# Patch tokens, two attentions and two mixtures of experts on one core: the turn to the second mixture laid out anew, LayerNorm factors in three parts, weight loads on another queue

## The reference, cut to what matters

```python
def reference(x, ...):                      # x: 128 images of 64 x 1000
    h = gelu(unfold(x, patch=(64, 25), stride=(64, 12)) @ tok_w + tok_b)   # 82 tokens of 64
    h = h + relu_attention(layernorm(h))    # causal, relu(q k^T) / row count
    h = h + moe6(layernorm(h))              # router MLP, top 2 of 6, three-layer experts
    h = h + rope_attention(layernorm(h))    # causal softmax, rotary part
    h = h + moe8(layernorm(h))              # top 2 of 8, out = tokens + sum of c_e * expert_e
    return h

def layernorm(x, eps=1e-5):
    return (x - mean(x)) / sqrt(var(x) + eps)

def moe8(tokens):
    rw, re = top_k(softmax(tokens @ router_w.T), 2)
    rw = rw / rw.sum(-1)
    return tokens + sum(combine[:, e] * (gelu(tokens @ w1[e] + b1[e]) @ w2[e] + b2[e]) for e in range(8))
```

## Time and profile before

| | us |
|---|---|
| median of 3 runs | 668.27 (664.47 to 670.48) |
| profiled execution | 667.97, its span 666.2 |
| TensorE busy | 591.1 (89% of the span) |
| VectorE busy | 505.0 (76%) |
| ScalarE busy | 297.6 (45%) |
| GpSimd busy | 148.0 (22%) |
| mean granted TensorE clock | 0.959 of full |

### The profile page before, as it was taken

How to read it: one execution, slowest core, us unless ns; L and a number is a source line. 1 busy time by engine, 2 the same in 40 slices (tenths; PEclk the granted TensorE clock), 3 DMA queues, 4 the chain that set the end, 5 groups by cost and what they waited for, 6 DMA issues and landing times.

```text
span 666.2 us, 17580 instructions
## 1 busy us (share of the span) xinstructions
PE 591.1 (89%) x6943; PEld 369.3 (55%) x6943; DVE 505.0 (76%) x1493; ACT 297.6 (45%) x716; POOL 148.0 (22%) x151
## 2 busy tenths in 40 slices
PE   1899999899998799999988889999967879999883
PEld 1885655468887344445443358777764444444441
DVE  3657779848785769888787548878887888988863
ACT  0010010023334466776775648887852434545441
POOL 1000000853655103221011041531421122121000
PEclk9999999999989799999998999999975899999997
DMA  9999883000000000000000000000000000000001
GB/s 296 411 384 331 292 292 132 2 1 1 2 1 2 1 1 1 3 1 1 2 1 1 1 2 1 1 2 2 1 1 1 7 16 22 22 22 21 20 22 25
DMA packets 28898, 39.19 MB, mean 59 GB/s; under 512 B 19985, under 2 KB 20369, under 8 KB 28817
## 3 DMA queue, kind: packets, MB, share of 16 engines
q1 hardware_dynamic: 19232, 35.46, 15.0%
q10 hardware_dynamic: 9584, 2.61, 2.0%
HBM read 35.37 MB, written 2.69 MB: 57 GB/s over the span
## 4 chain that ended last, share of the span: by engine, by line
PE 55%; DVE 24%; issue 7%; ACTq 6%; ACT 5%; DMA 2%; SPq 0%; DVEq 0%
PE bank L1522 8%; PE bank L403 7%; ACTq L1192 6%; DVE m_hm L1783 4%; PE bank L1560 4%; PE bank L1042 2%; PE bank L1558 2%; PE bank L1583 2%; PE bank L992 2%; PE bank L1006 2%; PE bank L1543 2%; PE bank L785 2%; PE bank L771 2%; DVE cols L446 2%; PE bank L1532 2%
## 5 line engine op out<-in xcount | busy, mean ns | idle before, releaser
L558 POOL TENSOR_TENSOR centred<-h,mean 82x512 f32<-82x512 f32 x64 | 72.8, 1137 | 447.3 <-DVE rstd L541 236.9
L1403 ACT ACTIVATE m_h<-bank,m_b 128x656 f32<-128x656 f32 x112 | 90.5, 808 | 115.6 <-PE bank L1522 115.4
L403 PE MATMUL bank<-cols,tok_weight 64*64 64x328 f32 (+1 forms) x1800 | 114.8, 410 | 20.2 <-DVE cols L447 18.3
L1783 DVE TENSOR_TENSOR m_hm<-bank,m_h 128x656 f32<-128x656 f32 x112 | 93.7, 836 | 34.3 <-PE bank L1532 33.0
L403 PEld LDWEIGHTS bank<-cols,tok_weight 64*64 64x64 f32 x1800 | 75.4, 135 | 55.1 <-issue 17.5
L1522 PE MATMUL bank<-m_xt,m_w 64*64 64x328 f32 x896 | 92.5, 485 | 5.9 <-ACT m_h L1403 5.0
L446 DVE COPY cols<-image 128x1992 f32<-128x1992 f32 x32 | 62.0, 1945 | 16.9 <-DMA image<-in_x_dram 14.8
L1558 PE MATMUL bank<-m_hm,m_wo 64*64 64x328 f32 x512 | 49.3, 455 | 2.7 <-DVE m_osb L1790 2.3
L1522 PEld LDWEIGHTS bank<-m_xt,m_w 64*64 64x64 f32 x896 | 24.8, 137 | 45.8 <-issue 23.2
L952 ACT ACTIVATE sa_prob<-sa_masked,sa_low 82x82 f32<-82x82 f32 x128 | 44.6, 350 | 11.3 <-DVE sa_low L1094 11.2
L381 ACT ACTIVATE tok_fm<-bank,tok_bias 128x328 f32<-128x328 f32 x16 | 7.6, 532 | 88.9 <-PE bank L403 63.1
(11 more groups left out here) (170 smaller groups left out, 1026.0 us busy)
## 6 DMA issues: line engine op xcount, KB each, us to landing
image<-in_x_dram SPq DMA_DIRECT2D x32, 1000.0 KB, 11.1
out_dram<-m_fin SPq DMA_DIRECT2D x16, 164.0 KB
tok_weight<-in_L_tok_weight_dram ACTq DMA_DIRECT2D x2, 400.0 KB, 8.1
m_w<-in_L_ffn_w_dram ACTq DMA_DIRECT2D x2, 128.0 KB
m_sel_raw<-c_sel_dram ACTq DMA_DIRECT2D x1, 256.0 KB
m_w<-in_L_ffn_expert_w_dram ACTq DMA_DIRECT2D x2, 96.0 KB
m_wo<-in_L_ffn_expert_w_dram ACTq DMA_DIRECT2D x4, 48.0 KB
m_sel_raw<-c_sel_dram ACTq DMA_DIRECT2D x1, 192.0 KB
```

The costliest lines, as they stand in the source:

```text
L403: return pe.matmul(sum_bank[u % 2][s][t * D:(t + 1) * D, L * j0:L * j1], weight[s * R:(s + 1) * R, c, :], cols[u % 2][s * R:(s + 1) * R, c ...
L558: pool.tensor_tensor(self.centred[:], slots(self.h, g), mean.broadcast_to([L, G, D]), ALU.subtract).then_inc(self.shifted, 1)
L1403: act.activation(h1[n % RING][:], h1_bank, ACT.Gelu if last else ACT.Relu, bias=W.b1[:, k:k + 1]).then_inc(h1_ready, 1)
L1783: dve.tensor_tensor(hm[k][:], cb_bank, src[n % RING][:], ALU.mult).then_inc(hm_ready, 1)
```

## The change

Nothing that is computed changes but the Newton steps' form. In words:

1. **Loads**: both mixtures' weight DMAs (54) go from ScalarE's queue to SyncE's, behind all image loads. `prepare` of both goes to VectorE's unit 7, ahead of `store(6)`.
2. **LayerNorm**: `scale` in three parts (groups 0 to 7, 8 to 11, 12 to 15), 14 instructions each, one third-order step and one Newton step, some without a wait. Every group counts by itself. In R and S the parts are spread over more groups; M does parts 1 and 2 of its own and 0 and 1 of S's; N does parts 1 and 2 of its own.
3. **Boundary S to N**: N's early turns go to banks 0, 2, 3, 2, 0 and wait for S's last `copy_qk`; the queues are interleaved anew; `copy_p` of the last group goes to ScalarE; S's last three groups' statistics go into N.
4. **Routing in N**: another `ROUTE`, and a `FIRST_ROUTE` for group 0.

```diff
@@ build
-            norm.append(LayerNorm(..., norm[-1] if i else None))
+            norm.append(LayerNorm(..., norm[-1] if i else None, (NG // 2, 3 * NG // 4, NG)))
@@ scalar queue
                 for f in range(3):
                     go(n, 1)
                     go(s, 2)
+                go(n, 1)
                 go(s)
                 go(n)
@@ tensor queue
                 go(s, 2 * (NG - 3) + 1)
                 go(n, 1)
                 go(s, 2)
+                for _ in range(2):
+                    go(n, 1)
+                    go(s, 1)
                 go(n, 1)
-                go(s, 1)
-                go(n, 1)
-                go(s, 1)
+                go(s, 2)
                 go(n, 1)
                 go(s, 1)
                 go(n, 1)
@@ vector queue
                 go(s, 2 * (NG - 2) + 1)
                 go(n, 1)
+                go(s, 3)
+                go(n, 1)
                 go(s, 1)
-                go(n, 1)
-                go(s, 2)
                 go(n, 1)
@@ stage_patches
         in_groups(step)
+        for W in moe:
+            W.load(sp)
...
-            for W in LOAD_IN.get(u, ()):
-                (*attn, *moe)[W].load(act)
+            if u == 0:
+                for W in attn:
+                    W.load(act)
...
+            if u == NU - 1:
+                for W in moe:
+                    W.prepare(dve)
             if u >= 1:
                 store(u - 1)
...
-            if u in PREPARE_IN:
-                moe[PREPARE_IN.index(u)].prepare(dve)
-            if u in (4, 5):
+            if u in SCALE_IN:           # (5, 6)
                 go(scale, 3)
+        go(following.scale(dve, 1))
@@ LayerNorm.scale(self, dve, part)
+        dve.wait_ge(self.counted, end)
         if self.previous is not None:
-            dve.wait_ge(self.previous.normed, NG if half else NG // 2)
+            dve.wait_ge(self.previous.normed, end)
+        self.mark(q = stats2 + EPS * D + stats5)
         self.link(d = even - odd)
+        yield
+        self.mark(mean = -0.5 * d + even)
         self.link(var = d * n * n / D / D * d)
         self.link(var = q / D + var)
         yield
         (two bit instructions on d)
+        yield
+        self.link(q = d * d); self.link(q = q * var)
+        yield
+        self.link(q = (q - 10/3) * q); self.link(d = (q + 5) * d)
+        yield
+        self.link(q = d * d); self.link(q = q * -0.5 * 0.375**3 * var); rstd = (q + 1.5 * 0.375) * d
@@ stage_relu_attention (vector); the rope attention has 1 <= g <= 6 in place of 2 <= g <= 7
-            if 1 <= g <= 3:
-                go(scale_mine, 2)
-            if 9 <= g <= 10:
-                go(scale_next, 3)
+            if 2 <= g <= 7:
+                go(scale_mine, 1)
+            if 9 <= g <= 11:
+                go(scale_next, 2)
@@ stage_rope_attention
+        copy_p(NG - 1)                                  # scalar, last
-                pe.wait_ge(S.behind.x_ready, g + 5 - NG)
+                pe.wait_ge(S.behind.x_ready, 1)
             if g == NG - 2:
+                yield
                 score(NG - 1)                           # tensor
         turn_p(NG - 1)
+        yield
         mix(NG - 1)
             if g == NG - 1:
                 copy_p(NG - 2)                          # vector
+                yield
-            if exists(g - 2):
+            if 2 <= g < NG - 2:
                 statistics(g - 2)
-        copy_p(NG - 1)
-        statistics(NG - 2)
@@ stage_moe
     if last:
-        ROUTE = {(0, 0): (1, 2), (0, 1): (3,), (0, 2): (4,), (1, 0): (5, 6), (1, 1): (7,), (1, 3): (0,)}
+        ROUTE = {(0, 0): (1,), (0, 1): (2,), (0, 3): (3, 4), (1, 0): (5,), (1, 1): (6, 7), (1, 3): (0,)}
+        FIRST_ROUTE = {(0, 0): (0,), (0, 1): (1, 2), (0, 3): (3, 4)}
+        SCALE_MINE, SCALE_NEXT = ({(0, 2): 2, (1, 2): 2, (2, 2): 2}, {(3, 2): 2, (4, 3): 2, (5, 2): 2}), ()
+        COUNT = {(0, 3): NG - 2, (2, 3): NG - 1}
     else:
+        SCALE_MINE = {(g, k): 1 for g in (1, 2) for k in range(NP)}, {(g, k): 1 for g in (4, 5) for k in range(NP)}
+        SCALE_NEXT = {(g, k): 1 for g in (10, 11, 12) for k in (0, 1)}, {(g, k): 1 for g in (NG - 2, NG - 1) for k in range(NP)}
+        COUNT = {(0, LAST): NG - 1}
...
-        return back if last and f <= FRONT else front
+        return psum[:, (0, 2, 3, 2, 0)[f], :] if last and f <= FRONT else front
...
-                pe.wait_ge(before.scaled, NG - 4 + f)
-                wait(pe, x_ready, f)
+                if f in (0, FRONT):
+                    pe.wait_ge(before.scaled, NG if f else NG - 4)
+                elif f < 3:
+                    pe.wait_ge(before.qk_ready, NG)
+                else:
+                    pe.wait_ge(x_ready, 2)
...
         if last:                                        # tensor
             turn(0)
             yield
+            turn(1)
+            yield
             pe.wait_ge(before.v_ready, NG)
             logits(0)
-            turn(1)
-            yield
+            yield
+            turn(2)
             logits(1)
-            yield
-            turn(2)
             yield
             logits(2)
             turn(3)
             yield
             logits(3)
+            pe.wait_ge(x_ready, FRONT)
             layer1(0, 0)
+            yield
             turn(FRONT)
...
+        if last:                                        # vector
+            route(0, 0)
+            route(0, 1)
+            take_logits(2)
+            yield
+            route(0, 2)
+            take_logits(3)
+            route(0, 3)
+            route(0, 4)
+            yield
+            for k in range(5, 8):
+                route(0, k)
+            count(NG - 4)
+            count(NG - 3)
```

128 lines of the change are left out of this document (62 added, 66 removed).

## The result

The changed kernel takes 673.12 us (median of 20 runs, 668.97 to 675.56), the kernel before 667.19 (20 runs, 659.06 to 672.61). The ratio is 1.0116, with a 95% interval of 1.0089 to 1.0143. The prediction had 650.5 and a range of 641 to 664. The profiled execution of the changed kernel took 670.68 us (span 668.9), 2.7 us over that of the kernel before, and 2.4 under its own median, so the traces show less than half of the difference of the medians (5.9 us). A ratio compares executions of both kernels that ran beside each other and leaves out those over 1.5% above the fastest of their kernel (6 of 20 here, all of the kernel before), so it is not the quotient of the two medians.

What follows compares the result with a forecast made beforehand. The prediction took TensorE's gaps in bounded places, worst at S to N, and the slow clock after them as the bound. Terms 2.3 + 2.4 + 1.3 + 1.3 + 9.4 + 1.1 = 17.8 us off 667.97 gave 650.2, stated 650.5, range 641 to 664.

Steps and rivals of the forecast that it cites:

- Part 1: End of tokenising: moving loads and `prepare` removes 5.3 us of TensorE gaps, costs 3, nets +2.3 us (5.3 to -9).
- the meeting with GpSimd: End of tokenising: GpSimd stretches VectorE's small operations; charged 3 us together with the late landing.
- the landing: End of tokenising: last weights arrive at about 134 us, where up to 131.6 costs nothing; 134 costs 2.4 us.
- Part 2: LayerNorm `scale` in three parts: gains of 2.4 us in R, 1.3 in M and 1.3 in S.
- The boundary: S to N: reordered queues gain 13.4 us by the walk, less 4 for the clock: +9.4 us (5 to 12).
- The walk: S to N: new queues followed stepwise from `turn_p(13)`, gaining 13.4 us at full clock; first `spread` after 18.6 us, before 26.5.
- the 4 us for the clock: S to N: charge for TensorE's clock falling again, for less long, after 6 to 7 us of gaps (2 to 8).
- the sign of being right: S to N: the slow clock was to last under 12 us in place of 27.
- the first rival: S to N: the slow clock stays, the boundary keeps 5 us, time 654.6, up to 660; chance 0.15.
- N: Routing and rest of N: 2.6 us from weighing in time, less 1.5, booked +1.1 us (-1 to 3).
- the late scale part: In N: the `scale` part at groups 3, 4 and 5 was to cost 1.5 us.
- The rival that ended slower: End of tokenising: `prepare` and VectorE's queue wait for weights; 678 us at 1.1 us per load; chance 0.06.

Runs made afterwards that it cites:

- e2: Changed kernel with GpSimd's first normalise held until both `prepare` are done, loads still on SyncE; ratio 1.0014 to the kernel before.
- e16: Kernel before, plus four repeated sets of eight products in TensorE's waits at the first boundary (R to M); ratio 0.9954 to the kernel before.
- e5: Changed kernel with the first scale part for R back in units 4 and 5; ratio 0.9997 to the kernel before.
- e6: e5 with the second scale part for R also moved into R's groups 1 to 3; ratio 0.9982 to the kernel before.
- e3: Kernel before with only the weight loads moved to SyncE and both `prepare` in the last unit; ratio 0.9987 to the kernel before.
- e1: Changed kernel with weight loads back on ScalarE and both `prepare` back in units 4 and 5; ratio 0.9952 to the kernel before.
- e4: Changed kernel with S's scale in halves, the second half computed in S, not M's last two groups; ratio 1.0021 to the kernel before.
- e14: e10 with M's own scale in halves as before; ratio 0.9856 to the kernel before.
- e11: Changed kernel with N's routing back in its old slots; ratio 1.0173 to the kernel before.
- e10: Changed kernel with R's first scale part in units 4 and 5, its second in R, and S's scale in halves; 659.16 us, ratio 0.9900 to kernel before.
- e12: e10 plus five repeated sets of small products in TensorE's waits at the boundary S to N; ratio 0.9840 to the kernel before.

## Why the prediction was wrong, step by step

- **Part 1, booked at +2.3, is the step that failed**: "I put 3 us for both", the meeting with GpSimd and the landing. It measured 10.4 us lost where 2.3 were to be gained. Landing and issue time (30.1 us) were right, and the wait for the last weights is 2.1 us (e2). TensorE's gaps did vanish, but the 5.3 us for them rest on one trace: that of e16 has 2.1 us of them in the same code. The 20 operations grew by 11.7 us, and the two new waits of TensorE brought its clock to half besides. I had sized the meeting by one row (0.95 us for L529) and not multiplied it by the operations that would stand beside GpSimd. And I had seen that "GpSimd starts only behind the last copy" and booked it as a gain, without asking what stands on VectorE at that time: the very operations that part 1 moves there. Moving the scale back by one unit wins 7.6 us, and its second part out of the way another 5.3 (e5, e6). Without the scale's changes part 1 ends 2.2 us earlier (e3), without part 1 those changes end 0.8 later (e1), both within the 2.2 us by which traces of one code differ; together they cost 10.4. The rule that the prediction quotes from the Trainium skill's "SBUF — State Buffer", section "Who interferes with whom", was the better guide, and I took a smaller price against it; even its "about zero" was too mild, because it left out the scale part and the clock. The prediction also reads from the earlier trace rows that the longest issues are those of the transposed loads. The rows do not bear this out (two `m_wr` took 4.20 us, 2.10 each, and the one `m_w`, which is not transposed, 2.65), and on SyncE's queue, with the image traffic over, a transposed `m_b` or `m_wr` takes 0.63 to 0.66 us and `m_w` 0.60 to 0.73.
- **Part 2.** R gained 2.7 (booked 2.4), but in part by luck: behind the same wait (1.52 us for 1.51) the clock stayed at 1.00 in the traces of e3 and e16, which have R as before and take 64.6 us for it, so 0.9 of the 2.7 is a slow stretch that the one trace of the kernel before had; I had booked 1.6 for it. S gained 1.2 (booked 1.3). M, booked at +1.3 (2 less 0.5 is 1.5) with a low end of -1.5, lost 6.3: 5.3 in the last two groups (e4), where I had costed nothing although the change puts six pieces with fourteen operations there, and 1.0 in the rest (e14: 0.9). Here too two small operations met GpSimd right ahead of the `weigh` that TensorE waits for.
- **The boundary, booked at +9.4.** The walk was right (18.6 us against 18.65 with the clock held up) and the 4 us for the clock were not: it took back 5.6 of the walk's 7.9 up to the first `spread`, and stayed at half for 24 us where under 12 was the sign of being right. That was the first rival, with 0.15. By undoing it the reorder is worth 1.6 us.
- **N, booked at +1.1**, gained 2.6 in its last twelve groups, which is the 2.6 of my count without the 1.5 that I took off for the late scale part; the routing as a whole gained 4.0 by the trace of e11, a part of which I had booked under the boundary.
- **Not booked at all**: the first boundary, 2.3 us in this trace. In the other runs that share its code it is 21.8 to 25.9, by where the clock falls, so it is no gain of the change; 22.5 is at the low end, and the trace of the kernel before is 3.1 us longer than that of e16 up to the end of R, in the same code; both may be why the traces differ by less than the medians, which was not tested.
- The rival that ended slower had the wrong mechanism: VectorE's queue was late, as it said, but not by waiting for weights.

## What to carry to other kernels

Before small operations are moved to another engine's idle time, list what GpSimd does at that time *after all parts of the change*, and multiply the drawn-out duration (here 0.9 to 1.1 us for 0.2) by the number of operations that meet it; then look which wait they stand ahead of. Try the parts of a change one by one and in pairs: here each of two groups of edits alone moved the end of tokenising by no more than traces of one code differ (e3, e1), and together they cost 10.4 us. Read a gap or a slow stretch in a second trace of the same kernel before booking its removal: 5.3 us of gaps were 2.1 in another. And where TensorE waits in a few bounded places, filling the waits with idle products can be worth more than shortening them (4 to 4.6 us a boundary, against 1.6 for the new order).

## What was not expected of the hardware

- Repeated products with no use made the kernel faster: 4 us at one boundary, in the old code and in the new, with a granted clock of 1.00 (2.4 GHz) where it had been 0.50 (1.2 GHz).
- Code that is the same, behind the same waits, kept full clock in one kernel and not in the next (R of e10 and e12: 64.92 and 68.12 us). A term of 3 us at a boundary is within what this moves. Elsewhere the stretches repeat closely: M's first ten groups took 99.67 to 99.74 us in eleven of these kernels (99.89 and 99.96 in two more).
- GpSimd's clearing of tiles, one behind the other, can hold a one-source VectorE operation through eight of them (4.63 us for 0.18 in e1); in the changed kernel three such operations got through the same run of clearings in 2.38, 0.83 and 1.33 us. A two-source one beside them took its usual time: in e3 L1243 at 132.79 took 0.28 us while `rh` was being cleared. The Trainium skill's "SBUF — State Buffer", section "Who interferes with whom", says of operations with two SBUF inputs that they contend only with a GpSimd instruction that reads SBUF; these rows agree (the prediction had left that condition out), and in e1 the other side is held through a run of GpSimd instructions, not through one.
